# Later reciprocals, earlier turned maxima and another order of SP's issues in a gated cross-attention and mixture-of-experts layer

## What is computed

```
def _L0_xattn_ref(x1, x2, Wq, bq, Wk, bk, Wv, bv):
    ...
    scores = jnp.einsum('bhqd,bhkd->bhqk', q, k) / jnp.sqrt(jnp.asarray(D_HEAD, dtype=q.dtype))
    attn = jax.nn.softmax(scores, axis=-1)
    out = jnp.einsum('bhqk,bhkd->bhqd', attn, v)
    ...
x = x + jnp.tanh(g_xattn[0]) * _L0_xattn_ref(_layernorm(x, axis=-1), ctx_2048, ...)
x = x + jnp.tanh(g_ffn[0]) * _L0_ffn_ref(_layernorm(x, axis=-1), ...)
```

## Time and profile before

| | us |
|---|---|
| median of three executions | 1432.28 |
| lowest and highest | 1427.72, 1443.97 |
| the profiled execution | 1418.35 |
| its span, first to last instruction | 1416.5 |
| TensorE busy in the span | 1333.9 (94%) |
| VectorE busy | 984.4 (69%) |
| ScalarE busy | 872.6 (62%) |
| GpSimd busy | 868.1 (61%) |

### The profile page before, as it was taken

One profiled execution on the slowest core, in us unless ns is written; L12 is line 12 of the kernel. 1 busy time (PEld: TensorE's weight loads), 2 busy tenths in 40 slices (PEclk: granted clock), 3 DMA queues, 4 the chain that ended last, 5 costly groups with the idle time before them and its releaser, 6 DMA issues.

```text
span 1416.5 us, 24632 instructions
## 1 busy us (share of the span) xinstructions
PE 1333.9 (94%) x7290; PEld 648.6 (46%) x7290; DVE 984.4 (69%) x1661; ACT 872.6 (62%) x1720; POOL 868.1 (61%) x1278
## 2 busy tenths in 40 slices
PE   3899999999999999999999998899999999999997
PEld 1222223222222322222232232377787888888886
DVE  4888889998798988988899988556654333333332
ACT  2488788788687877777787886724334333333433
POOL 7447667768687877777788864542213555555553
PEclk8799999999999999999999999999999999999999
DMA  6567676676676767676766763366554788786655
GB/s 174 159 183 220 188 215 210 187 208 198 170 192 196 200 180 193 214 182 178 200 205 188 196 181 104 101 218 154 136 186 81 195 217 207 175 198 110 114 106 81
DMA packets 161309, 247.90 MB, mean 175 GB/s; under 512 B 33605, under 2 KB 58828, under 8 KB 161182
## 3 DMA queue, kind: packets, MB, share of 16 engines
q1 hardware_dynamic: 142926, 208.96, 51.6%
q0 software_dynamic: 18256, 37.38, 14.2%
HBM read 141.32 MB, written 103.88 MB: 173 GB/s over the span
## 4 chain that ended last, share of the span: by engine, by line
PE 61%; DVE 13%; issue 10%; DMA 6%; SPq 4%; POOL 3%; POOLq 1%; ACT 1%; DVEq 0%; ACTq 0%
PE m_banks L950 20%; PE bank L907 12%; PE bank L878 11%; DVE row_max L1123 9%; PE m_banks L857 7%; PE bank L838 4%; PE bank L894 2%; DMA arena<-parts_q 2%; DMA arena<-arena 2%; PE bank L883 2%; PE bank L842 2%; POOL xs L781 2%; SPq L470 2%; SPq L531 1%; PE bank L972 1%
## 5 line engine op out<-in xcount | busy, mean ns | idle before, releaser
L1123 DVE TENSOR_REDUCE row_max<-m_banks 128x2 f32<-128x1024 f32 x512 | 614.6, 1222 | 68.9 <-PE m_banks L857 63.5
L1395 ACT ACTIVATE arena<-bank 128x512 f32<-128x512 f32 x1024 | 556.2, 606 | 101.7 <-PE bank L878 96.9
L878 PE MATMUL bank<-arena 112*128 112x512 bf16 x1024 | 314.8, 386 | 2.4 <-ACT arena L1395 1.5
L907 PE MATMUL bank<-arena 128*32 128x512 f32 x2048 | 277.3, 613 | 0.4 <-ACT arena L1403 0.4
L793 POOL DMA_INDIRECT out<-xs,ids x71 | 112.5, 1584 | 172.9 <-ACT xs L1470 137.9
L857 PE MATMUL m_banks<-arena 48*128 48x512 bf16 x1024 | 169.9, 393 | 47.1 <-DVE row_max L1123 34.6
L878 PEld LDWEIGHTS bank<-arena 112*128 112x128 bf16 x1024 | 79.7, 100 | 247.0 <-ACT arena L1395 88.5
L950 PE MATMUL m_banks<-w_ring,h_hi 128*128 x568 | 183.1, 403 | 0.0
L1459 ACT ACTIVATE arena<-m_banks 128x256 f32<-128x256 f32 x103 | 39.5, 384 | 188.7 <-PE m_banks L950 188.6
L857 PEld LDWEIGHTS m_banks<-arena 48*128 48x128 bf16 x1024 | 39.8, 93 | 185.2 <-issue 87.2
L950 PE MATMUL m_banks<-w_ring,h_lo 128*128 x284 | 111.7, 393 | 0.0
(11 more groups left out here) (176 smaller groups left out, 2047.9 us busy)
## 6 DMA issues: line engine op xcount, KB each, us to landing
pv_d<-arena SPq DMA_DIRECT2D x32, 512.0 KB, 4.3
w_ring<-split_d SPq DMA_DIRECT2D x60, 256.0 KB, 3.9
parts_k<-arena SPq DMA_DIRECT2D x96, 128.0 KB
parts_q<-arena SPq DMA_DIRECT2D x96, 128.0 KB
arena<-parts_k SPq DMA_DIRECT2D x64, 192.0 KB
arena<-parts_q SPq DMA_DIRECT2D x64, 192.0 KB
arena<-in_w SPq DMA_DIRECT2D x36, 256.0 KB, 7.0
arena<-in_ctx SPq DMA_DIRECT2D x32, 256.0 KB, 3.4
```

Of the source, the lines that this page charges most:

```text
L878: nc.tensor.matmul(out, k_stack[b % 3][0:SHIFTED, h, kt * P:(kt + 1) * P], q_stack[b % 3][0:SHIFTED, h, :], start=True, stop=True).then_in ...
L907: last = nc.tensor.matmul(pv_ps[2 * DH * j:2 * DH * (j + 1), :], v_ones[b % 3][:, kt, GROUP * g + j, :], probs[pair % 3][:, j, :], start=( ...
L1123: nc.vector.reduce_max(pair, m_ps[(STEPS * b + u) // 2 % M_PAIRS], AX_X).then_inc(s_mx, 1)
L1395: nc.scalar.activation(probs[group % 3][:, j, :], bank_of["scores", b, s], ACT.Exp, scale=float(DH) ** -0.5).then_inc(s_exp, 1)
```

## The change

The reciprocals are made at step 16 of VectorE's turn instead of 11. On TensorE the turned maxima are issued in front of the value block instead of behind it. On SP the six reads of the query come first, then the store of the reciprocals, then the row of maxima of the next batch; and the high key part is written in front of the staged weights' stores, the middle and low parts behind them as before. On GpSimd the low part of the staged weights is made behind the scatters.

```diff
--- before.py
+++ after.py
@@ -63,7 +63,7 @@
 LOGITS_AT = 16
 MOMENTS2_AT = 10
 MOMENTS_AT = 27
-RECIP_AT = 11
+RECIP_AT = 16
 GROUP = 4
 EXPERTS = 8
 FF = 256
@@ -543,29 +543,31 @@
                     read(i + 2, 0)
                     write(i + 2, 1, MID)
                     write(i + 2, 1, LO)
-                if is_b(i - 1):
-                    store_reciprocals(i - 1)
                 if is_b(i + 4) and i + 4 >= 2:
                     load_ctx(i + 4)
                 if is_b(i - 3):
                     store_turned(i - 3)
+                if is_b(i + 2):
+                    read(i + 2, 1)
+                if is_b(i - 1):
+                    store_reciprocals(i - 1)
                 if is_b(i + 1):
                     row(i + 1, 0)
-                if is_b(i + 2):
-                    read(i + 2, 1)
                 if is_b(i - 1):
                     load_values(i - 1)
                 if is_b(i - 2):
                     store_tokens(i - 2)
                 if is_b(i + X_AHEAD):
                     load_x(i + X_AHEAD)
+                if is_b(i + 3):
+                    write(i + 3, 0, HI)
                 if 0 <= i + 2 < len(STAGED):
                     store_staged(i + 2)
                 if 0 <= i + 3 < len(STAGED):
                     load_staged(i + 3)
                 if is_b(i + 3):
-                    for part in (HI, MID, LO):
-                        write(i + 3, 0, part)
+                    write(i + 3, 0, MID)
+                    write(i + 3, 0, LO)
                 for r in SHARED_ROWS.get(i, ()):
                     if r == 2:
                         sp.wait_ge(s_sst, 2 * DMA * len(STAGED))
@@ -750,11 +752,11 @@
                     normalise(i + 4)
                 if is_b(i - 2):
                     tokens(i - 2)
-                if 0 <= i + 2 < len(STAGED):
-                    staged_low(i + 2)
                 for b in range(B - 2 * CHUNK):
                     if i == min(b + 10, B - 1):
                         scatter(b)
+                if 0 <= i + 2 < len(STAGED):
+                    staged_low(i + 2)
                 if is_b(i + 3) and i + 3 > 0:
                     split(i + 3, 0)
                 if is_b(i - 1):
@@ -1000,14 +1002,14 @@
                     if is_b(i):
                         exp_scores(i, s + 2)
                         exp_scores(i, s + 3)
+                    if s + 3 == MAX_AT[1] and is_b(i):
+                        turn_maxima(i, 1)
+                    if s + 3 == MAX_AT[0] and is_b(i + 1):
+                        turn_maxima(i + 1, 0)
                     if s == 0 and is_b(i - 1):
                         values(i - 1, STEPS // GROUP - 1)
                     if s and is_b(i):
                         values(i, s // GROUP - 1)
-                    if s + 3 == MAX_AT[1] and is_b(i):
-                        turn_maxima(i, 1)
-                    if s + 3 == MAX_AT[0] and is_b(i + 1):
-                        turn_maxima(i + 1, 0)
                     if s + 3 == COUNT_SLOT and i >= 7 and (i - 7) % CHUNK == 0:
                         count_choices((i - 7) // CHUNK)
                     if i == B - 1 and s == FIRST_JOB_AT:
```

## The result

The changed kernel took 1472.13 us (median; 1469.57 to 1473.1), the kernel before on the same chip 1430.0 (1426.54 to 1443.97): a ratio of 1.0273, with the 95% interval [1.0202, 1.0344]. On a second chip it was 1467.93 against 1424.71 us, 1.0322 [1.0273, 1.0371]. It is slower by some 3%. The forecast was 1425 us and a range up to 1446. What came true is rival 2, and more of it than rival 2 gave.

The account below looks back on a forecast made before the run. SP's queue ring was taken to bind after the change, eating most of the 18 and 6 us that VectorE's edits free; stretches 0, -3.1, -2.5 and start -1.0 gave about -7 us: 1425 from 1432.28, range 1400 to 1446.

Parts of the forecast that it names:

- rival 2: SP's wait for the reciprocals' landing gets no relief; ring 29.4 us at worst, decisive from 28.6; 1446 to 1460, chance 0.15.
- The named loop: SP's ring from key read to key read: 25.80 us before, forecast 26.6 in the first stretch, 27.5 in the second.
- Key read to query reads, 8.5 us: Ring's first piece on SP: 8.50 us until the query parts are written and landed.
- Query reads to value load, 3.87 + 3.4 us: Ring's middle piece on SP: 3.87 us issuing six reads, then 3.4 us until the reciprocals' store lands.
- The relief, 1.7 us: Value load to next key read on SP: an empty queue saves 3.5 - 1.8 us net; bounds none and 3.5.
- The sum: Stretches of 10, 15 and 5 attention batches: 0, -3.1 and -2.5 us, start -1.0, together -6.6, say -7 us.
- Query reads in front of the row: On SP, reads no longer wait for the row of maxima: nothing to 1.2 us gained a batch in the first stretch.
- The start: At the kernel's start the query reads go some 2.4 us earlier and 0.96 us of idle time goes: 1.0 us gained.
- Reciprocals at step 16, 18 us: On VectorE, the 13.7 us wait before the reciprocal goes; with TensorE's stalls and clock 18 us, if nothing else limits.
- Turned maxima first, -6 us: On TensorE, the transpose ahead of the value block frees about 12 us of VectorE, half given to TensorE: 6 us.
- Scatters in front of the low parts, and the high key part: zero: Reordering on GpSimd is zero, at most 0.3 us a batch both ways; the earlier key write on SP zero.
- The floor of 26.1 us past batch 6: Batch length with TensorE practically never idle: 25.56 us, nearer 26.1 past the sixth batch because of VectorE's routing chains.

Follow-up runs that it names:

- e1: Changed kernel with SP's queue put back as it was before, the other edits kept: 1424.63 us, ratio 0.9899 to the kernel before.
- e4: Changed kernel with the reciprocals' store in front of the query reads again, the row still behind them: 1444.77 us, ratio 1.0034 to the kernel before.
- e14: Changed kernel with the row in front of the query reads again, the reciprocals' store still behind them: 1475.28 us, ratio 1.0357 to the kernel before.
- e2: Kernel before with the new order of SP's queue alone: 1473.53 us, ratio 1.0228.
- e3: Changed kernel with the scatters behind the low parts again: 1478.37 us, ratio 1.0238 to the kernel before.
- e13: Kernel before with the reciprocals at step 16 and the high key part written in front of the staged stores: 1403.16 us, ratio 0.9878.
- e5: Kernel before with the reciprocals at step 16 and nothing else: 1402.46 us, ratio 0.9852.
- e16: Kernel before with the reciprocals at step 16 once more, on a second chip: 1401.26 us, ratio 0.9819.
- e8: Kernel before with the reciprocals at step 16 and the turned maxima in front of the value block: 1410.8 us, ratio 0.9915.
- e11: Kernel before with the scatters starting in turn 18 instead of 10: 1435.16 us, one execution, 26.80 us a batch in turns 11 to 16.
- e9: Changed kernel with SP's old queue order, and the three key writes in front of the staged stores and load: 1420.86 us, ratio 0.9991 to the kernel before.
- e12: Changed kernel with the load of the values moved behind the key writes on SP: 1541.24 us, ratio 1.0863 to the kernel before.
- e17: Changed kernel with the reciprocals' store in front of the query reads and the scatters begun in turn 18: 1443.08 us, one execution.
- e10: Changed kernel with the scatters starting in turn 18 instead of 10: 1486.64 us, one execution, 27.95 us a batch in turns 11 to 16.

## Why the prediction was wrong

**The mechanism was right, its size and its chance were not.** The named loop, the store behind six reads, SP waiting for its landing, the load of the values behind that and the key parts behind the load, is what the time went into: the chain of after runs through it, and e1, e4 and e14 turn the loss off and on with the store's place. I gave it 27.5 us and rival 2 a chance of 0.15; it has 29.9. The prediction's own sign of rival 2, marks over 28.5 us apart, is there past batch 10 (29.8).

**Key read to query reads, 8.5 us.** Measured 8.3 and 8.5.

**Query reads to value load, 3.87 + 3.4 us.** Right in the first stretch: 7.5, with the load 3.1 to 3.7 us behind the reads. Wrong in the second: 8.8, with the load 3.5 to 7.7 us behind them. The failed step here is that I took the same landing with scatters in flight. The store's landing in after, in turns 1 to 9 and then in turns 10 to 24 (the whole of before had 1.4/3.1/4.2):

```profile
DMA to landing us min/median/max: 3.0/3.3/3.6
```
```profile
DMA to landing us min/median/max: 3.4/4.7/7.6
```

In before the store is sent in front of the scatters and lands after 2.7 to 3.7 us in the second stretch too, so its row could not show this. The fit in the Trainium skill (DMA: Bandwidth & Descriptors, Anatomy of one DMA) would make it 2.04 us, as the prediction said; the page gives it for a DMA that GpSimd issues, this one is SP's, and the trace says 3.3 and 4.7 at the median.

**The relief, 1.7 us.** This is the step that failed first and that weighed most: (13.43 - 1.7) and (12.57 - 1.7). In the first stretch value load to key read is 12.5 us, as in before (12.5): no relief at all, though the queue in front of the load was empty. In the second it is 12.6 instead of 14.1, but that is no relief either: in e2 and e3, with the scatters where they were, it is 14.1 and 14.0 and the middle piece 7.4 and 7.6. The scatters' cost only changed its piece. By this term alone the first stretch is 1.6 us a batch longer than forecast. What it rested on, that the values queue behind 3.6 us of reads, was read off the queue, and no row showed a load that landed earlier behind an empty one. The chain shows what the piece is made of instead: SP's issues from the load to the last key write, 6.7 us at the mean in the first stretch, and that write's landing, 5.8 us; in before 6.3 and 6.2. Neither waits for the values to land. The lower bound, none, was the value.

**The sum.** First stretch: ring 28.3 instead of 26.6, batches 27.9, 275.4 us instead of 261.6. Second: 29.9 instead of 27.5, 447.2 us instead of 413. Third: 28.1 us a batch instead of 26.3, 140.6 us instead of 131.5; that nothing is to be loaded there saved no microsecond against after's own first stretch. Rival 2's line of decision, a ring of 28.6 us, was passed in the second stretch and nearly met in the first; its end of 29.4 us was passed in the second too. Its price was short as well: 15 x 1.1 + 6 x 1.0 = 22.5 us (which turns -7 into +15.5, not +14) is for the ring only, and the clock was only named. Of the 31.1 us of the second stretch 11.0 are busy time of TensorE at a lower clock.

**Query reads in front of the row.** I saw in it only a gain of up to 1.2 us for the reads, and priced the row's own delay at nothing. In the first stretch that is right (e4: 26.3 us). From batch 10 on it is wrong: e4 against e1 is 1.3% or some 20 us, and both differ only by the place of row and high key part, the latter worth zero by e13. The start, priced at -1.0 us, won nothing: the mark is at 56.06 and was at 56.02.

**Reciprocals at step 16, 18 us.** Right as to mechanism and size: the wait of the earlier trace rows is gone, e5 gives 22 us (0.9852, interval -0.8 to -2.1%), e16 23 us.

**Turned maxima first, -6 us.** Wrong in sign: +8 us (e8 against e5). The wait on VectorE's side went away as said. I feared the bank of the logits, with its cover of 0.2 us, and gave it no price; there the transpose never waited. I wrote that the half at step 0 gains nothing; it is the half that loses most, 0.27 us a batch against 0.19 at step 16, and only there does the transpose wait for its bank.

**Scatters in front of the low parts, and the high key part: zero.** Right (e3, e13).

**The floor of 26.1 us past batch 6.** In turns 11 to 16 both e11 (before without scatters) and e5 (with them, and the reciprocals at step 16) take 26.8 us, so that nothing tried here comes down to 26.1. The 28.2 us of before in these turns are, by the same traces, the early reciprocal and the scatters together, which I had seen as something that GpSimd hides.

**Together.** On one scale: reciprocals -22, turned maxima +8, which leaves e8, and e1 (on another chip) says the same with 0.9899 beside 0.9915. SP's order lies on top of that: 1.0273 over 0.9899 is 1.038, 54 us, of which the row from batch 10 on has some 20 and the store 34 (after over e4, 1.0273 over 1.0034 is 1.024). With the row back in front (e14) the store alone has the whole loss, so these two do not add up: whichever is later hides the other. In the kernel before, without the gains, SP's order costs 33 us (e2), and after is no faster than e2 (1.0273 and 1.0228, with intervals that overlap): the 14 us that the other edits win in e1 do not get through the longer loop.

**What stays open.** That the loss goes through SP's ring (1a) rests on the chain of after and e14. No experiment takes 1a away and leaves 1b: e9 shows only that the ring has room in the old order, and e12 built a loop of its own. How long a batch of after would be by the late sum alone is not known. Open is also why the landings come late with scatters in flight.

## What to carry to other kernels

A store whose landing the same queue waits for belongs in front of other work, not right in front of its waiter: look for the pair, and count all that stands between. Behind six reads it put 3.4 us of waiting into each turn of SP's ring, and the batches grew by 1.6 us in the first stretch and 2.5 in the second (after against e1). No relief came from the queue being empty afterwards; a relief that no row shows is to be taken as zero. Small stores and loads that someone waits for should stand far ahead of their use as soon as indirect scatters are in flight, and a term measured ahead of them must not be used behind them. When waits contradict each other between two runs, follow the chain over the stretch in question. In this bundle of edits the one constant was the whole gain, so try edits one by one.

## What the runs showed of the hardware

With GpSimd's indirect scatters in flight (two a batch), small transfers of SP's queue that are sent beside them report their end late. The reciprocals' store in after lands 3.0 to 3.6 us after its issue in turns 1 to 9 and 3.4 to 7.6 us in turns 10 to 24; the row's second DMA in e4 goes from 2.5 to 4.1 us to 6.1 to 10.7 us. Sent in front of the scatters, as in before, the store stays at 2.7 to 3.7 us. In one such spell, 565.0 to 570.9 us of after, the trace has no DMA packet at all, so this delay is not one of bandwidth. What does delay it isn't settled by these runs. That the scatters are the condition is shown by moving them: in e17 they start at turn 18, and in turns 11 to 16 TensorE does not stall on the row and a batch takes 26.85 us, where e4 has 29.41.

Scatters made a batch 1.7 us longer in after (e10) and 2.6 us in e4 (e17), each by one execution. In e5, whose small transfers stand ahead of the scatters and whose reciprocal comes late, a batch with them takes the 26.8 us of e11 without them.

TensorE's stall of 1.12 us in the earlier trace rows was followed by 3.4 us at a granted clock of 0.50. In the stall of 5.71 us that ends at 570.95 the clock fell at 568.3, with TensorE idle since 565.2, and stayed at 0.50 for 6.8 us. In the attention of after the low stretches add up to 57.8 us, in before to 20.4; TensorE's busy time grew by 11.0 us in the second stretch.
